# Attention block on one core: output product fed by f16 parts that a transposing transfer turns, in place of f32 parts turned on TensorE

## The reference

```
h = maximum(layernorm(x), 0)
q, k, v = h @ Wq.T, h @ Wk.T, h @ Wv.T            # each split in 16 heads of 32
a = q . k * 512**-0.5 + (adj + adj)               # per head, 256 x 256
a = where(a row has a nonzero, a, -inf);  p = softmax(a), nan -> 0
out = x + (p . v, heads side by side) @ Wo.T
```

## Time and profile before

| what | value |
|---|---|
| time, median of 3 runs (lowest to highest) | 1252.07 us (1252.06 to 1252.55) |
| the profiled execution: its time, and the span of its instructions | 1249.15 us, 1247.4 us |
| TensorE busy | 1209.6 us (97%) |
| VectorE, ScalarE, GpSimd busy | 1088.7 (87%), 1029.7 (83%), 905.8 (73%) |
| mean granted share of TensorE's clock | 0.997 |
| transfers | 179.90 MB in queue 1, 59.6% of the 16 DMA engines' time |

### The profile page before, as it was taken

How to read it: one execution, slowest core, us unless ns; L and a number is a source line. 1 busy time by engine, 2 the same in 40 slices (tenths; PEclk the granted TensorE clock), 3 DMA queues, 4 the chain that set the end, 5 groups by cost and what they waited for, 6 DMA issues and landing times.

```text
span 1247.4 us, 42107 instructions
## 1 busy us (share of the span) xinstructions
PE 1209.6 (97%) x12856; PEld 1087.1 (87%) x12856; DVE 1088.7 (87%) x3500; ACT 1029.7 (83%) x2398; POOL 905.8 (73%) x1268
## 2 busy tenths in 40 slices
PE   6899999999999999999999999999999999999997
PEld 5788988888889888889888888888898888898896
DVE  7798888888888888888888888898888888888887
ACT  5788888888888888888888888888888888888886
POOL 5587777777777777777677777777777777776775
PEclk9899999999999999999999999999999999999999
DMA  6567555676656676565775565765556755556643
GB/s 227 122 143 166 140 129 142 141 174 150 146 120 146 151 169 149 134 139 138 161 169 135 121 154 135 177 154 135 127 148 149 170 144 135 137 137 169 146 106 90
DMA packets 157431, 181.73 MB, mean 146 GB/s; under 512 B 80641, under 2 KB 90369, under 8 KB 157313
## 3 DMA queue, kind: packets, MB, share of 16 engines
q1 hardware_dynamic: 157312, 179.90, 59.6%
HBM read 46.14 MB, written 16.78 MB: 50 GB/s over the span
## 4 chain that ended last, share of the span: by engine, by line
issue 49%; POOL 45%; POOLq 2%; DVE 2%; PE 1%; DMA 1%; ACT 0%; SPq 0%; DVEq 0%
POOL fold L1117 14%; POOL o_raw L1091 6%; POOL bounds L1123 6%; POOL y L1109 6%; POOL mask L1084 3%; POOL o L1097 3%; POOL h L1076 2%; POOL factor L1088 2%; POOL rstd L1065 2%; PE job_ps L374 1%; DMA x_in<-x 1%; POOL minus_mean L1060 1%; POOL var_eps L1062 0%; POOL wo_lo L1130 0%; POOLq L1119 0%
## 5 line engine op out<-in xcount | busy, mean ns | idle before, releaser
L1117 POOL TENSOR_TENSOR fold<-minus 128x512 f32<-128x512 f32 x256 | 327.2, 1278 | 247.5 <-DVE bounds L901 247.5
L681 ACT ACTIVATE probs<-minus,bounds 128x256 f32<-128x256 f32 x1024 | 464.6, 508 | 28.3 <-DVE bounds L901 28.2
L910 DVE TENSOR_TENSOR pT_lo<-pT_ps,pT_hi 128x512 f16<-128x512 f32 x512 | 350.0, 684 | 90.0 <-ACT pT_hi L692 85.9
L901 DVE CUSTOM_DVE_ANT_0 minus<-s_ps,adj_now 128x256 f32<-128x256 f32 x1024 | 389.3, 418 | 6.3 <-ACT probs L681 4.6
L692 ACT ACTIVATE pT_hi<-pT_ps 128x512 f16<-128x512 f32 x512 | 306.2, 598 | 86.1 <-PE pT_ps L465 84.4
L374 PE MATMUL job_ps<-hT,w_hi 128*128 128x256 f16 x2048 | 350.5, 273 | 0.4 <-DVE hT L857 0.4
L465 PE MATMUL pT_ps<-ident,probs 128*128 128x128 f32 x2048 | 308.0, 273 | 1.8 <-ACT probs L681 1.6
L374 PE MATMUL job_ps<-hT,w_lo 128*128 128x256 f16 x1024 | 279.1, 273 | 0.0
L465 PEld LDWEIGHTS pT_ps<-ident,probs 128*128 128x128 f32 x2048 | 242.0, 141 | 19.2 <-ACT probs L681 2.5
L451 PE MATMUL s_ps<-qk_stack 96*128 96x256 f32 x1024 | 247.5, 323 | 5.1 <-DMA qk_stack<-qk_parts 5.1
L1123 POOL TENSOR_TENSOR bounds<-fold 128x256 f32<-128x256 f32 x256 | 197.6, 772 | 25.1 <-POOL fold L1117 9.6
(11 more groups left out here) (92 smaller groups left out, 1835.3 us busy)
## 6 DMA issues: line engine op xcount, KB each, us to landing
qk_stack<-qk_parts SPq DMA_DIRECT2D x756, 128.0 KB, 2.3
x_in<-x SPq DMA_DIRECT2D x32, 512.0 KB, 4.8
x_res<-x SPq DMA_DIRECT2D x32, 512.0 KB, 3.9
out<-y SPq DMA_DIRECT2D x64, 256.0 KB, 2.1
adj_in<-adj SPq DMA_DIRECT2D x32, 256.0 KB, 3.5
qk_stack<-qk_parts SPq DMA_DIRECT2D x24, 64.0 KB, 2.0
w_in<-wq SPq DMA_DIRECT2D x2, 512.0 KB, 5.6
w_in<-wk SPq DMA_DIRECT2D x2, 512.0 KB, 6.4
```

The costliest lines, as they stand in the source:

```text
L681: end = nc.scalar.activation(probs[hh % 2][:, t, :], minus[hh // 2 % 2][:, hh % 2, t, :], ACT.Exp, bias=bounds[:, hh // 2 % 4, 2 * (hh % 2 ...
L901: end = nc.vector.tensor_tensor_reduce(out=minus[pair % 2][:, hh % 2, t, :], in0=s_ps[SCORE_BANK[hh]][:, t * N:(t + 1) * N], in1=adj_now[: ...
L910: nc.vector.tensor_tensor(pT_lo[hh % 4][:, :, :], pT_ps[hh % 2][:, :].rearrange("p (m n) -> p m n", m=NT), pT_hi[hh % 4][:, :, :], ALU.sub ...
L1117: nc.gpsimd.tensor_tensor(f1[:, :, :], src[:, :, 0:N // 2], src[:, :, N // 2:N], ALU.add).then_inc(folded1, 1)
```

## The change

`o` is no longer turned on TensorE (except for the last batch's first half). ScalarE makes its high part in f16 where it lies (`high_outputs`, end of slot 14 for columns 0 to 255, end of slot 3 of the next batch for the rest), VectorE the low part (`low_outputs`, end of slots 15 and 4), both into `o_parts`, and SyncE turns the two parts with one transposing transfer for each half (`turn_outputs`): the first half at the end of a batch's transfers, the second half between `j` = 1 and `j` = 2 of `stack(1, b)`. The output product has f16 operands. So that the parts of `Wo` fit f16, the first batch now measures the largest entry (`out_weight_extent`, `out_weight_top`, one more transpose on TensorE, `out_weight_scale`), GpSimd scales `Wo` (`level_out_weight`), and the factor is put back when `y` is taken.

`JOBS` moves `y` 0 from slots 4 and 5 to 8 and 9 and `qk` 0 and `qk` 1 of the next batch from slots 6 to 9 to slots 4 to 7; the banks alternate in the new order. Beside this: `low_tokens(b + 2, 0)` goes from slot 11 to 14, `split_tokens` from 10 to 11, the statistics of both token halves to slot 7; both stores of `y` go behind `stack(0, b + 1)` and `turn_tokens(b + 2, 0)`; each half of `stack` has semaphores of its own; in the first batch `load_tokens(2)` and the second `turn_tokens(1, 1, ...)` are placed otherwise around `stack(1, 0)`.

```diff
     2: [("v", 2, 0, 2, 12), ("v", 3, 0, 0, 3)],
-    3: [("v", 3, 0, 3, 12), ("o", 1, -1, 0, 4)],
-    4: [("y", 0, -1, 0, 6)],
...
+    3: [("v", 3, 0, 3, 12)],
+    4: [("qk", 0, 1, 0, 12)],
...
+    8: [("y", 0, -1, 0, 6)],
+    9: [("y", 0, -1, 6, 12)],
...
-    13: [("y", 1, -1, 6, 12), ("o", 0, 0, 0, 4)],
+    13: [("y", 1, -1, 6, 12)],
...
+FIRST_JOBS = {**JOBS, 4: [], 5: [], 6: JOBS[4], 7: JOBS[5], 8: JOBS[6], 9: JOBS[7], 12: [], 13: []}
+
+LAST_JOBS = {**{hh: [j for j in JOBS[hh] if j[2] < 1] for hh in JOBS}, 13: JOBS[13] + [("o", 0, 0, 0, 4)]}
...
-        wo_hi, wo_lo = sb("wo_hi", [P, KT, D], F32R), sb("wo_lo", [P, KT, D], F32R)
+        wo_hi, wo_lo = sb("wo_hi", [P, KT, D], F16), sb("wo_lo", [P, KT, D], F16)
...
-        oT_hi = sb("oT_hi", [P, KT, N], F32R)
-        oT_lo = sb("oT_lo", [P, KT, N], F32R)
+        o_parts = sb("o_parts", [P, 2, NT, 2, HALF], F16)
+        oT = [sb(f"oT{n}", [P, NT, 2, 2, P], F16) for n in range(2)]
...
                     for r, pair in enumerate((slice(1, 3), slice(0, 3, 2), slice(1, 4, 2))):
                         sp.dma_start(qk_stack[HD * r:HD * (r + 1), half, j, :, :, :].bitcast(F32),
                                      qk_parts[HD * j:HD * (j + 1), half, pair, :, :].bitcast(F32)
-                                     ).then_inc(stacked[j], 16)
+                                     ).then_inc(stacked[half][j], 16)
+                    if first and j == 0:
+
+                        turn_tokens(1, 1, 1, True)
+                    if half == 1 and j == 1 and not first:
+
+                        turn_outputs(b - 1, 1)
...
+            def turn_outputs(b, n):
+
+
+                sp.wait_ge(o_split, b * 2 + (n + 1))
+                settled(sp, "sp")
+                sp.dma_start_transpose(oT[n][:, :, :, :, :].rearrange("p t a k c -> p (t a k) c"),
+                                       o_parts[:, n, :, :, :].rearrange("p t a d -> p (t a d)")
+                                       ).then_inc(o_turned[n], 16)
...
                 stack(1, b, first)
-                if not first:
-                    store(b - 1, 0)
+                if first:
+                    load_adj(1)
                 if not last:
                     stack(0, b + 1, False)
                 if not ends:
                     turn_tokens(b + 2, 0, odd, False)
                 if not first:
+                    store(b - 1, 0)
                     store(b - 1, 1)
 
                     sp.dma_start(x_res[:, :, :], x_d[b]).then_inc(res_loaded, 16)
+                if not last:
+                    turn_outputs(b, 0)
...
                     if n == 0 and start == 0:
 
-                        pe.wait_ge(taken["o"], count("o", 0, b + d))
+                        pe.wait_ge(o_turned[0], (b + d + 1) * 16)
                     if n == 0 and start <= half < stop:
 
-                        pe.wait_ge(taken["o"], count("o", 1, b + d))
+                        pe.wait_ge(o_turned[1], (b + d + 1) * 16)
...
+            def high_outputs(b, n):
+
+
+                act.wait_ge(o_ready, b * QUADS + 2 * (n + 1))
+                nc.scalar.activation(o_parts[:, n, :, 0, :], o[:, :, n * HALF:(n + 1) * HALF], ACT.Copy
+                                     ).then_inc(o_high, 1)
...
+            def low_outputs(b, n):
+
+                dve.wait_ge(o_high, b * 2 + (n + 1))
+                settled(dve, "dve")
+                nc.vector.tensor_tensor(o_parts[:, n, :, 1, :], o[:, :, n * HALF:(n + 1) * HALF], o_parts[:, n, :, 0, :],
+                                        ALU.subtract).then_inc(o_split, 1)
...
-                        if hh == 3:
-                            tokens_stats(b + 2, range(0, 1))
-                        if hh == 6:
-                            tokens_stats(b + 2, range(1, NT))
-                            moments_of(b + 2, 2 * (b + 2))
-                        if hh == 11:
+                        if hh == 7:
+                            tokens_stats(b + 2, range(NT))
+                            moments_of(b + 2, b + 3)
+                        if hh == 14:
                             low_tokens(b + 2, 0)
+                    if not first and hh == 4:
+                        low_outputs(b - 1, 1)
+                    if not last and hh == 15:
+                        low_outputs(b, 0)
...
+                if quad % 2 == 0 and not first:
+
+                    pool.wait_ge(o_split, b * 2 - 1 + quad // 2)
```

More of the change, by code:

```diff
@@ L61, in jobs_at @@
 def jobs_at(hh, first, last):
-    return [j for j in JOBS[hh] if not (first and j[2] < 0) and not (last and j[2] > 0)]
+    return (FIRST_JOBS if first else LAST_JOBS if last else JOBS)[hh]
 def ended_before(hh, first, last):
@@ L308, in _ @@
                 first_stack(n)
-            for t in range(NT):
-                turn_tokens(1, t, 1, True)
+            load_tokens(2)
+            turn_tokens(1, 0, 1, True)
             def body(b, odd, first, last):
                 ends = last or isinstance(b, int) and b + 2 == B
-                if not (last or isinstance(b, int) and b + 2 == B):
+                if not (first or ends):
                     load_tokens(b + 2)
@@ L577, in last_product @@
                     pe.wait_ge(last_taken, 2)
-                end = product(job_ps[bank("y", n, B - 1)][:, :], [lambda k, v=v: v[:, k, n * P:(n + 1) * P] for v in oT],
+                end = product(job_ps[bank("y", n, B - 1)][:, :], [lambda k, a=a: oT[k // 2][:, n, a, k % 2, :] for a in range(2)],
                               [lambda k, w=w: w[:, k, :] for w in (wo_hi, wo_lo)], start, stop)
@@ L743, in body @@
                         take("v", 3, b, first)
+                    if hh == 14 and not first:
+                        take("y", 1, b - 1)
                     if hh + 1 < HEADS:
@@ L761, in body @@
                         split_tokens(1, True)
-                    if not (nearly or last) and hh == 10:
+                    if not first and hh == 3:
+                        high_outputs(b - 1, 1)
+                    if not (nearly or last) and hh == 11:
                         split_tokens(b + 2, False)
+                    if not last and hh == 14:
+                        high_outputs(b, 0)
             body(0, True, False, False)
@@ L873, in take @@
                 elif kind == "o":
-                    nc.vector.tensor_tensor(oT_lo[:, 2 * n:2 * n + 2, :], ps[:, :].rearrange("p (k n) -> p k n", k=2),
-                                            oT_hi[:, 2 * n:2 * n + 2, :].bitcast(F32), ALU.subtract).then_inc(taken["o"], 1)
+                    for t in range(NT):
+                        end = nc.vector.tensor_tensor(oT[0][:, t, 1, :, :],
+                                                      ps[:, :].rearrange("p (k n) -> p k n", k=2)[:, :, t * P:(t + 1) * P],
+                                                      oT[0][:, t, 0, :, :], ALU.subtract)
```

125 lines of the change are left out of this document (92 added, 33 removed), and 5 rows, old and new, of the table JOBS.

## The result

The changed kernel takes 1291.16 us (median of 4 runs, 1287.51 to 1293.73) against 1252.31 us of the kernel before (4 runs beside it, 1252.06 to 1252.76). The ratio is 1.031, 95% interval 1.028 to 1.0335: slower by 39 us, where 26 us of gain were forecast. The profiled execution took 1287.51 us, its span is 1285.7 us, TensorE's mean granted clock 0.993 of full speed.

A forecast was written before the change was run, and what follows sets the result against it. Bound by TensorE, with little lead over VectorE: floor 35.66 plus 1.45 us of stalls is 37.1 us a batch, 0.8 less; 26.1 us in all, so 1223.1 profiled, 1226 us median, range 1202 to 1245.

The forecast's parts named there:

- The floor: TensorE's own list per batch: 36.90 us less 0.88 for transposes of `o` and 0.36 for f16 matmuls, 35.66 us.
- Rival D: Output product: f16 is no faster, losing 11 us over all, 1237 us; counted inside the forecast's range, without its own chance.
- the one on transfers: Slot 7: the second turned half delays the stack's later transfers, stalling TensorE 0.9 us, or 0.4 if slot 2 loses 1.1.
- Slot 7's term: TensorE waits in slot 7 for the stack's third transfer after the turned half: 0.4 to 0.9 us a batch.
- Rival B: Nothing gained: both stalls at their upper bound, with batch-start transfers delaying `j` = 0; 2.25 us stall, 1250 us, chance 0.09.
- VectorE's step: Around a batch's start VectorE runs late, stalling TensorE in slot 2 by 1.1 us, or 0.2 without waiting for GpSimd.
- the case without waits for GpSimd: VectorE at a batch's start: `low_probs` 1 ends at 5.8, so slot 2 stalls 0.2 us; both stalls together 1.1.
- Rival C: SyncE's list held up in slot 4 by late `low_outputs`; 3.3 us stall a batch, 1281 us, chance 0.08.
- The ends: First batch gains 3.5 us (0 to 4.9); last batch costs +1 us (-1 to +3).
- The 4.89 us wait: First batch, slot 5: TensorE waits for the stack, which now goes ahead of two transfers; 3.5 us of gain given.

The follow-up runs named there:

- e2_no_turn: Changed kernel without the two transposing transfers of the attention output (the output product reads zeros): 1243.12 us, ratio 0.992 to the kernel before.
- e11_narrow: Changed kernel with the first half of `low_outputs` on 4 of 256 columns of each token tile, the rest left zero: 1287.71 us (one run).
- e13_plain_copy: Changed kernel with its two output transfers as plain copies of the same bytes, so the product reads wrongly ordered numbers: 1271.08 us, ratio 1.016.
- e7_all: Changed kernel, `low_tokens` slot 11, `low_outputs` 14, statistics 6 and 7, second half turned behind stack, first turned and stored before batch's end: 1250.86 us, ratio 0.9985.
- e3_turn_after_stack: Changed kernel with the second half of the output turned behind the stack's twelfth transfer, not its sixth: 1274.26 us, ratio 1.017.
- e12_last_y: Changed kernel with the first part of `y` 0 in slot 4, not 8, in the last batch only: 1279.84 us (one run).
- e15_last_spread: Changed kernel with the last batch's first part of `y` 0 split over slots 5 and 7 instead of slot 8: 1282.59 us (one run).
- e9_low_0: Changed kernel, `low_tokens` slot 11, statistics 6 and 7, first `low_outputs` in next batch's slot 0, both halves turned behind stack: 1229.59 us, ratio 0.981.
- e5_low_14: Changed kernel with `low_tokens` in slot 11, and first-half `low_outputs` in slot 14 with its ScalarE half in 13: 1289.66 us, ratio 1.030.

## Why the prediction was wrong

**The floor** was right: 35.5 us measured, 35.66 forecast; the f16 step is 0.216 (0.217 forecast), the transposes of `o` and the wait for a bank in slot 4 are gone. Against 36.90 it is 1.4 us a batch of real gain, 42 us over 30 batches. Rival D is out.

**The step that failed is the one on transfers.** It gave the stack its old start, 6.5 us behind the batch's, and a queue with nothing in its way: the first half unharmed, every transfer landing 2.3 us after its issue, and only slot 7 at risk, 0.4 to 0.9 us. Slot 7's term came out (0.66 us); what was put at nothing, the first half of the stack, costs 1.34 us in slots 4 to 6. The third transfer lands 2.95 us later than before. Some 1.3 us of it is the stack's start: the take of `qk` 3 is in the VectorE list that the prediction itself laid out as late, but its lateness was carried to slot 2 alone. The other 1.6 us is the landing, 4.1 us after the issue and not 2.5. The median 2.3 us was one over 756 transfers, most of which leave when the engines are free; one crowded stretch, batch 15 of before, would have given 2.8 for the first five. The issue of the first turned half (1.29 us) is counted nowhere either; e2_no_turn, where it is gone, starts the stack no sooner, so alone it costs nothing there, but it is what holds the stack in e11_narrow. e2_no_turn takes 1.7 of the 2.07 us of slots 4 to 8 away by taking out the two transfers, and e13_plain_copy shows that the bytes and the waits for them weigh more than the turning. Rival B named this delay, at `j` = 0, and left 0.35 us for it (2.25 less 1.9).

**VectorE's step** was right in kind and too large in size: slot 2 loses 0.70 us (1.1 forecast), as `h_parts` in slot 14 took 0.84 (1.5 forecast), since it began ahead of `y`, while `low_outputs` in slot 15 took 1.38 (0.9). The sum has a slip besides: with 0.9 and 0.3 us less for the two instructions `low_probs` 1 ends at 5.5, not at 5.8, so that the case without waits for GpSimd has no stall in slot 2. By the rule of the Trainium skill (SBUF — State Buffer, "SBUF: two separate sides") such an instruction and one of GpSimd's that reads SBUF exclude each other for the whole instruction; e11_narrow, where 155 ns of work take 0.85 us and end with `fold`, agrees with it. What I missed are slots 14 (0.42 us) and 10 (0.20), where the same chain is late for other heads (in slot 10 with the token statistics in it, see e7_all); I had looked at two places only. In all 3.39 us are lost where 1.45 were forecast.

**Rival C** gave 1281 us and came near the time by luck. Its mechanism is there, SyncE waits for `low_outputs` 28 times, 23.3 us in all, and issues the second half at 12.9 and not 12.0; but e3_turn_after_stack, which takes them out of the stack's way, gives back only 0.19 us a batch.

**The ends.** The first batch was to gain 3.5 us and lost 4.2 with what lies ahead of it: slot 0 of batch 0 stands 1.8 us later, and a second stretch of half clock, 3.4 us long at 69.4, came in. The 4.89 us wait shrank as forecast, to two of 2.56 and 0.73 us, but slot 6 took most of that back: slots 4 to 9 of batch 0 are 0.5 us shorter, and slots 10 to 14, where the new stretch of half clock lies, 2.9 us longer. Variants put slot 0 of batch 0 anywhere from 31.0 to 32.2 us, so I take no cause from its place. The last batch lost 4.9 us, where +1 (-1 to +3) was forecast: waits for the stack, then half clock. The mechanism of the clock was in no step of mine.

**What stays open.** Whether thin work or waits lower the clock in the last batch (e12_last_y and e15_last_spread are single runs and remove neither cleanly, and other runs' last batches fit neither), and why the first batch is longer. What is shown: with the turned halves behind the stack and `low_outputs` away from GpSimd's work (e9_low_0), the kernel is 1.9% faster than the one before, 23 us. That this is near the 26 forecast is chance: it is another order of work, with 1.6 us of a batch still lost.

## What to carry to other kernels

Work that leaves a compute engine for a queue is not free because the queue has 40% of its time left: list what stands ahead of the next transfer that someone waits for, with its bytes and its issue, and take landing times from a stretch as crowded as the new one (here 3.9 us and not 2.4). Carry every lateness that you find on one engine to all that wait for that engine, the transfers too. Put the added transfers behind the urgent ones first. And place a VectorE instruction with two SBUF inputs where GpSimd is idle, for here it waited out the whole instruction that GpSimd was in (1.38 us and not 0.68).

## What the runs showed that I had not expected

A transposing transfer of 256 KB costs its queue 1.28 us of issue, a plain copy of the same bytes 0.53. A VectorE instruction of 8 elements in a row took 0.85 us beside GpSimd and 0.155 alone. In seven of the variants TensorE's clock was halved in mid-run too, 20 times between batch 1 and batch 30 (eight in e5_low_14; in e11_narrow at 205, 673 and 1062 us), each time from 0.4 us before to 1.5 us after the end of a TensorE wait of 1.8 to 2.7 us. Such a wait doesn't always bring it: the changed kernel has one of 2.7 us at 94 us and one of 1.9 us at 951 us, and kept full clock at both.
